# One drive of every second chunk goes from GpSimd to VectorE in a Mamba state-space loop

## The reference

```
xz = seq @ W_in.T ;  u, z = split(xz)
u = silu(causal_conv4(u) + conv_b)
dt = softplus(...) ;  Bmat, Cmat = rows of u @ W_x.T
h = exp(dt_t * A) * h + (dt_t * u_t) * B_t      # per channel and state
y = sum over states of h * C_t
out = (y + u * Dp) * silu(z) @ W_out.T
```

## Time and profile before

| | |
|---|---|
| median of 3 runs | 6102.17 us (6101.44 to 6105.2) |
| the profiled execution | 6112.24 us, span 6110.4 us |
| mean granted TensorE clock | 0.939 |
| state-space loop in the span | from about 75 to about 3714 us |
| busy over the span | PE 83%, DVE 80%, POOL 78%, ACT 55% |

### The profile page before, as it was taken

One profiled execution on the slowest core, in us unless ns is written; L12 is line 12 of the kernel. 1 busy time (PEld: TensorE's weight loads), 2 busy tenths in 40 slices (PEclk: granted clock), 3 DMA queues, 4 the chain that ended last, 5 costly groups with the idle time before them and its releaser, 6 DMA issues. The chain is left out here.

```text
span 6110.4 us, 72884 instructions
## 1 busy us (share of the span) xinstructions
PE 5081.1 (83%) x22486; PEld 2628.5 (43%) x22486; DVE 4908.9 (80%) x6708; ACT 3384.9 (55%) x4253; POOL 4779.0 (78%) x2219
## 2 busy tenths in 40 slices
PE   6888888888888888888888887972549989889897
PEld 2333333333433433433333334420326656566565
DVE  7999999999999999999999996006467677776665
ACT  4555565566566566555555552000437767667776
POOL 5999999999999999999999994000337767667676
PEclk8999999999999999999999998885879999999999
DMA  4555556555555555555555552681449999999999
GB/s 178 203 201 207 195 201 207 198 196 208 195 200 204 203 197 205 198 200 204 203 198 202 203 195 71 286 322 19 92 105 177 188 169 188 182 170 189 187 189 209
DMA packets 1424095, 1152.36 MB, mean 189 GB/s; under 512 B 1216728, under 2 KB 1226096, under 8 KB 1415792
## 3 DMA queue, kind: packets, MB, share of 16 engines
q1 hardware_dynamic: 1421330, 1149.30, 65.9%
q10 hardware_dynamic: 2528, 0.26, 0.0%
HBM read 814.23 MB, written 21.09 MB: 137 GB/s over the span
## 5 line engine op out<-in xcount | busy, mean ns | idle before, releaser
L871 POOL TENSOR_TENSOR mamba_state<-mamba_state,mamba_c_row 128x1024 f32<-128x1024 f32 x1024 | 2410.7, 2371 | 70.6 <-DVE mamba_state L831 62.5
L1750 POOL TENSOR_TENSOR l3s_el<-l3s_s_sb,l3s_eh 128x1024 f16<-128x1024 f32 (+2 forms) x584 | 1169.8, 2014 | 1121.0 <-ACT l3s_s_sb L1735 1113.5
L705 PE MATMUL mamba_y_ps<-mamba_state,ident 128*128 128x512 f32 x4096 | 1993.8, 613 | 40.6 <-POOL mamba_state L871 39.2
L831 DVE TENSOR_TENSOR_SCAN mamba_state<-mamba_decay,mamba_b_ps 128x1024 f32<-128x1024 f32 x704 | 1609.1, 2286 | 78.8 <-ACT mamba_b_ps L787 1.5
L705 PEld LDWEIGHTS mamba_y_ps<-mamba_state,ident 128*128 128x128 f32 x4096 | 780.4, 195 | 867.2 <-issue 681.1
L1758 DVE TENSOR_SCALAR_CACHE_REDUCE l3s_s_sb<-l3s_s_ps 128x512 f32<-128x512 f32 (+1 forms) x1096 | 753.5, 689 | 484.5 <-PE l3s_s_ps L1694 461.4
L1707 PE MATMUL l3s_o_ps<-l3s_vt,l3s_et 128*128 128x257 f16 x4368 | 878.3, 278 | 194.6 <-DMA l3s_et<-l3s_el 130.0
L1734 ACT ACTIVATE l3s_eh<-l3s_s_sb,l3s_shift 128x1024 f16<-128x1024 f32 (+2 forms) x584 | 634.5, 1087 | 541.8 <-DMA l3s_et<-l3s_el 441.3
L787 ACT ACTIVATE mamba_decay<-mamba_dt,mamba_A 128x1016 f32<-128x1016 f32 x704 | 791.7, 1133 | 235.5 <-POOL mamba_dt L852 167.0
L817 DVE TENSOR_TENSOR mamba_b_ps<-mamba_dtu,mamba_b_ps 128x1024 f32<-128x1024 f32 x704 | 850.8, 1209 | 30.8 <-PE mamba_b_ps L693 30.7
L693 PE MATMUL mamba_b_ps<-mamba_bc,mamba_pick 128*128 128x512 f32 x1408 | 571.9, 488 | 288.9 <-DVE mamba_state L831 282.2
(11 more groups left out here) (301 smaller groups left out, 5216.0 us busy)
## 6 DMA issues: line engine op xcount, KB each, us to landing
mamba_c_row<-mamba_c_rows SPq DMA_DIRECT2D x1024, 512.0 KB, 3.7
mamba_b_row<-mamba_c_rows SPq DMA_DIRECT2D x320, 512.0 KB, 4.8
l_ring_a<-in_L_conv_W SPq DMA_DIRECT2D x28, 1024.0 KB, 11.0
l2b_ring_b<-in_L_conv_W SPq DMA_DIRECT2D x26, 1024.0 KB, 11.1
mamba_xs<-X SPq DMA_DIRECT2D x64, 256.0 KB, 5.5
l_ring_a<-in_L_conv_W SPq DMA_DIRECT2D x14, 704.0 KB, 12.7
l2b_ring_b<-in_L_conv_W SPq DMA_DIRECT2D x13, 704.0 KB, 12.7
l_ring_a<-in_L_conv_W SPq DMA_DIRECT2D x14, 640.0 KB, 12.1
```

The costliest lines, as they stand in the source:

```text
L705: last = nc.tensor.matmul(y_ps[:, half(h)], C["ident"][:, :], state[:, s % STATES, half(h)], start=False, stop=(s == S - 1))
L831: nc.vector.tensor_tensor_scan(state[:, s % STATES, :], by, add, 0.0, ALU.mult, ALU.add).then_inc(s_scan, 1)
L871: nc.gpsimd.tensor_tensor(state[:, s % STATES, :], state[:, s % STATES, :], c_row[:, s % C_ROWS, :], ALU.mult).then_inc(s_hc, 1)
L1750: nc.gpsimd.tensor_tensor(el[:, part, off:off + EXPW], s_sb[:, par, j * EXPW:(j + 1) * EXPW], eh[:, part, off:off + EXPW], ALU.subtract).t ...
```

## The change

In odd chunks GpSimd's units are (2, 4, 6, 8) and no longer (2, 4, 6, 8, 10). Unit 10 of these 32 chunks is then made like any other of VectorE's: one-hot product on TensorE, drive on VectorE, decay into a `decay` tile. The one-hot blocks become twelve (`SPREAD`, the states that are VectorE's in some chunk). The counts that engines wait for go by a function `drives`, since the chunks no longer have equal numbers, and the row loads of slot 4 are counted per two chunks. To make room, `ImageNorm` keeps three slots in `norm_mine` and `norm_m2` instead of four, and `norm_var` shares the tile of `norm_minus`. The same instructions as before work on these.

```diff
-        self.mine = mem.sb("norm_mine", [P, B * G])
-        self.m2 = mem.sb("norm_m2", [P, B * G])
+        self.mine = mem.sb("norm_mine", [P, KEPT * G])
+        self.m2 = mem.sb("norm_m2", [P, KEPT * G])
...
-        self.var = mem.sb("norm_var", [P, G])
+        self.var = self.minus
...
+    def own(self, j):
+        return slice(j % KEPT * G, (j % KEPT + 1) * G)
...
-                for i, unit in enumerate(DVE_UNITS):
+                for i, unit in enumerate(SPREAD):
...
-POOL_UNITS = (2, 4, 6, 8, 10)
-DVE_UNITS = tuple(s for s in range(S) if s not in POOL_UNITS)
+POOL_UNITS = ((2, 4, 6, 8, 10), (2, 4, 6, 8))
+DVE_UNITS = tuple(tuple(s for s in range(S) if s not in units) for units in POOL_UNITS)
+SPREAD = tuple(s for s in range(S) if any(s in units for units in DVE_UNITS))
+
+
+def drives(units, c):
+
+    return (c + 1) // 2 * len(units[0]) + c // 2 * len(units[1])
...
-            return c * len(DVE_UNITS) + sum(1 for k in DVE_UNITS if k <= s)
+            return drives(DVE_UNITS, c) + sum(1 for k in DVE_UNITS[c % 2] if k <= s)
...
+        def b_loads(c, s):
+
+            return c + 1 if s in POOL_UNITS[1] else c // 2 + 1
...
-            if s in POOL_UNITS:
+            if s in POOL_UNITS[c % 2]:
                 return
             wait(pe, s_scan, unit + 1 - PAIRS)
...
-            if s in POOL_UNITS:
+            if s in POOL_UNITS[c % 2]:
                 wait(act, s_scan, unit + 1 - PAIRS)
...
         def dve_drive(dve, c, par, s):
-            if s in POOL_UNITS:
+            if s in POOL_UNITS[c % 2]:
                 return
...
-            wait(pool, s_brow[b_slot(s)], 16 * (c + 1))
+            wait(pool, s_brow[b_slot(s)], 16 * b_loads(c, s))
...
-            if s + B_LOAD_AHEAD in POOL_UNITS:
+            if s + B_LOAD_AHEAD in POOL_UNITS[c % 2]:
                 load_b(sp, c, par, s + B_LOAD_AHEAD)
...
-            if s + DRIVE_AHEAD in POOL_UNITS:
+            if s + DRIVE_AHEAD in POOL_UNITS[c % 2]:
                 pool_drive(pool, c, par, s + DRIVE_AHEAD)
```

More of the change, by code:

```diff
@@ L215, in vector_stats @@
     def vector_stats(self, dve, j):
-        nc, mine, m2 = self.nc, self.mine[:, self.groups(j)], self.m2[:, self.groups(j)]
+        nc, mine, m2 = self.nc, self.mine[:, self.own(j)], self.m2[:, self.own(j)]
         for g in range(G):
@@ L246, in scalar_stats @@
             act.wait_ge(self.s_first, G * (later + 1))
-            nc.scalar.activation(self.mine[:, self.groups(j)], self.sums[:, :], ACT.Identity,
+            nc.scalar.activation(self.mine[:, self.own(j)], self.sums[:, :], ACT.Identity,
                                  scale=0.5 / N).then_inc(self.s_centre, 1)
@@ L251, in scalar_stats @@
         wait(act, self.s_second, G * later + g)
-        at = j % B * G + g
+        at = j % KEPT * G + g
         nc.scalar.activation(over, group(g), ACT.Square, bias=self.minus[:, g:g + 1],
@@ L265, in sum @@
             src = (self.mine, self.m2)[k]
-            last = nc.tensor.matmul(ps[:, 0:G], self.C["one"][:, :], src[:, self.groups(j)], start=True, stop=True)
+            last = nc.tensor.matmul(ps[:, 0:G], self.C["one"][:, :], src[:, self.own(j)], start=True, stop=True)
         if k == 2:
@@ L310, in gpsimd @@
         nc, act_done, pool_done = self.nc, ACT_STEPS * j, POOL_STEPS * j
-        square, root, m2 = self.square[:, :], self.root[:, :], self.m2[:, self.groups(j)]
+        square, root, m2 = self.square[:, :], self.root[:, :], self.m2[:, self.own(j)]
         scale, bias = self.scale_g[:, self.groups(j)], self.bias_g[:, self.groups(j)]
@@ L314, in gpsimd @@
             pool.wait_ge(self.s_act, act_done + 1)
-            op = nc.gpsimd.tensor_tensor(self.dev[:, :], self.mine[:, self.groups(j)], self.mean[:, :], ALU.subtract)
+            op = nc.gpsimd.tensor_tensor(self.dev[:, :], self.mine[:, self.own(j)], self.mean[:, :], ALU.subtract)
         if i == 1:
@@ L333, in gpsimd @@
         op.then_inc(self.s_pool, 1)
-ACT_STEPS, POOL_STEPS = 10, 6
+ACT_STEPS, POOL_STEPS, KEPT = 10, 6, 3
 WEIGHTS = ("W_in", "conv_w", "conv_b", "W_x", "W_dt", "b_dt", "A_log", "Dp", "W_out")
@@ L608, in by_dve @@
         def by_dve(c, s):
-            return c * len(DVE_UNITS) + sum(1 for k in DVE_UNITS if k <= s)
+            return drives(DVE_UNITS, c) + sum(1 for k in DVE_UNITS[c % 2] if k <= s)
         def by_pool(c, s):
-            return c * len(POOL_UNITS) + sum(1 for k in POOL_UNITS if k <= s)
+            return drives(POOL_UNITS, c) + sum(1 for k in POOL_UNITS[c % 2] if k <= s)
         def b_slot(s):
-            return POOL_UNITS.index(s)
+            return POOL_UNITS[0].index(s)
+        def b_loads(c, s):
+            return c + 1 if s in POOL_UNITS[1] else c // 2 + 1
         def rows(h):
@@ L692, in pe_rows @@
             for h in range(2):
-                last = nc.tensor.matmul(b_ps[s % PAIRS][:, half(h)], C["pick"][:, DVE_UNITS.index(s) * P:(DVE_UNITS.index(s) + 1) * P],
+                last = nc.tensor.matmul(b_ps[s % PAIRS][:, half(h)], C["pick"][:, SPREAD.index(s) * P:(SPREAD.index(s) + 1) * P],
                                         bc[:, par, half(h)], start=True, stop=True)
@@ L741, in act_prep @@
                 wait(act, s_pbc, n + 1)
-                wait(act, s_b, len(DVE_UNITS) * (n - 1))
+                wait(act, s_b, drives(DVE_UNITS, n - 1))
                 nc.scalar.activation(bc[:, par, :], prep_ps[:, :], ACT.Copy).then_inc(s_hi, 1)
@@ L855, in pool_prep @@
                 wait(pool, s_u, n + 1)
-                wait(pool, s_drive, len(DVE_UNITS) * (n - 1))
-                wait(pool, s_bdrive, len(POOL_UNITS) * (n - 1))
+                wait(pool, s_drive, drives(DVE_UNITS, n - 1))
+                wait(pool, s_bdrive, drives(POOL_UNITS, n - 1))
                 nc.gpsimd.tensor_tensor(dtu[:, par, :], dt[:, par, :], u[:, :], ALU.mult).then_inc(s_dtu, 1)
         def pool_drive(pool, c, par, s):
-            if s == POOL_UNITS[0]:
+            if s == POOL_UNITS[0][0]:
                 wait(pool, s_dtu, c + 1)
-            wait(pool, s_brow[b_slot(s)], 16 * (c + 1))
+            wait(pool, s_brow[b_slot(s)], 16 * b_loads(c, s))
             row = b_row[:, b_slot(s), :]
@@ L970, in _ @@
                 for i in range(B_ROWS):
-                    sp.wait_ge(s_brow[i], 16 * TOTAL)
+                    sp.wait_ge(s_brow[i], 16 * b_loads(LAST, POOL_UNITS[0][i]))
             @block.tensor
@@ L2013, in program @@
         with Memory(nc, "mamba") as m:
-            C["pick"] = m.sb("pick", [P, len(DVE_UNITS) * P], fp32r)
+            C["pick"] = m.sb("pick", [P, len(SPREAD) * P], fp32r)
             Ms = [{"w_u": m.sb(f"w_u{i}", [P, TAPS * D]), "w_z": m.sb(f"w_z{i}", [P, D]), "w_dt": m.sb(f"w_dt{i}", [P, D]),
```

## The result

The changed kernel has a median of 6152.06 us (4 runs, 6146.53 to 6156.88) against 6101.81 for the kernel before (6100.37 to 6105.2): a ratio of 1.0084, 95% interval 1.0072 to 1.0095. It is slower by 50 us. The forecast was 6137 us, +35. The profiled execution took 6156.88 us, its span is 6155.1: 44.7 us more than the span before. (The profiled execution before lay 10 us above its median, that of after 5 us; hence 44.7 here and 50 there.)

What follows compares the result with a forecast made beforehand. VectorE's queue was taken to pace the state-space loop: added drives +35 us, its waits unchanged, everything else nothing, so 6137 us on the median of 6102.17. The range was 6110 to 6170 us.

Steps and rivals of the forecast that it cites:

- term for the drives: VectorE's added drive 10 in odd chunks: 31 x 1.12 us plus 0.3 in chunk 63, sum +35 us.
- VectorE's queue paces: State-space loop: VectorE's own queue sets the pace; GpSimd follows with no slack to spare but does not hold it.
- (A): Rival: GpSimd paces the loop and VectorE's waits are its lateness handed on; 6102 + 35 - 50 = 6087 us, chance 0.07.
- GpSimd's idling: GpSimd's idle before its products at L871 was to be about 180 us, against 70.6 before.
- Counts and norm tiles: Norm tiles kept for three images with one shared add no instruction or wait, and no cost: zero.
- ScalarE's earlier exponential: Unit 10's exponential goes into a decay slot, waiting for scan 6 instead of 8; nobody waits longer.
- the lighter DMA: SP's queue loses 32 row loads of 512 KB and their long-met wait: worth nothing.
- the twelfth one-hot copy: One more one-hot copy ahead of the loop, 0.2 us, counted as zero.
- I take them as unchanged: VectorE's 50 us of waits at drives, gate and scans stay as they are; bounds were -15 and +74 us.
- rival (C): Longer gap before z leaves TensorE at 1.2 GHz nearly every chunk: up to +74, 6176 us; half that excess 6156; chance 0.15.
- the gap before z: TensorE's idle before the z product at step 10 grows from 2.40 to about 2.95 us in odd chunks.
- The reason given for unchanged waits: Round trip from L805 to drive 11 against scan 10 is exactly the same; no row shows GpSimd's relief reaching the gate.

Runs made afterwards that it cites:

- e9: Kernel before, with one extra VectorE instruction ahead of u at step 4 of odd chunks, result to a free tile; 6148.57 us, ratio 1.0078.
- e4: Kernel before, with GpSimd's drive of unit 10 in odd chunks done on one column only, nothing added on VectorE; 6097.31 us, ratio 0.9992.
- e8: Change made twice: GpSimd has units (2, 4, 6, 8) in every chunk, against the kernel before; 6183.09 us, ratio 1.0129.
- e6: Changed kernel with two repeats of unit 11's one-hot product ahead of the z product at step 10; 6108.59 us, ratio 1.0007 to the kernel before.
- e10: Changed kernel with five GpSimd units in all chunks: all of the diff but the moved drive; 6104.21 us, ratio 1.0003 to the kernel before.
- e2: Changed kernel with the z product moved to step 11, behind unit 11's one-hot product; 6107.37 us, ratio 1.001 to the kernel before.
- e3: Changed kernel with a full-size GpSimd multiply on a free row replacing the lost drive in odd chunks; 6150.72 us, ratio 1.0083 to the kernel before.
- e5: Changed kernel, but VectorE takes over unit 8 instead of 10 in odd chunks; 6172.27 us, ratio 1.0114 to the kernel before.
- e11: Kernel before, with two repeats of unit 11's one-hot product ahead of the z product at step 10; 6076.38 us, ratio 0.9958.
- e1: Kernel before, with the z product moved from step 10 to step 11, behind unit 11's one-hot product; 6080.66 us, ratio 0.9966.

## Why the prediction was right, and where it fell short

The direction, its mechanism and the range held: +50 us against +35, within 6110 to 6170. The term for the drives was right to about 1 us; the term for VectorE's waits was not.

- VectorE's queue paces: shown. e9 adds 37 us of another instruction to it and costs 45; e4 takes 71 us from GpSimd and brings 4. With (A), GpSimd as the pace, e4 would have been at 6052.
- A drive ahead of L805 costs 1.12 us: 57.09 for an undisturbed chunk in e8 against 55.97, and in e6 even and odd chunks differ by 1.13. In the changed kernel itself only three odd chunks have no wait; they take 57.21 to 57.27.
- GpSimd's idling, forecast at about 180 us, is 184.8.
- Counts and norm tiles: zero, by e10. ScalarE's earlier exponential, the lighter DMA and the twelfth one-hot copy were not tried by themselves. The profile after shows no wait of VectorE for DMA in the loop's chunks, and for ScalarE 0.5 us, against 2.5 before.
- **The step that failed is "I take them as unchanged"**, of VectorE's 50 us of waits. In the profiled executions the waits at drive 11 grew from 30 to 51 us and those at the gate fell by 13; with those before scans the sum rose by 6. The first is rival (C), of which I had taken the upper end as 39 us more and gave 0.15. It came true by half. The second I had put at nothing. That +35 came as near as it did is in part luck: two errors of opposite sign. Filled (e6) or reordered (e2), the changed kernel loses 43 to 45 us of its time.
- The profile before understates the rise, since it was a long execution. e10 runs the same schedule as the kernel before, and its profile (6099.61 us) has 46.1 us of waits from first scan to last, where the change has 59.1: +13. With the 36 of the drives this makes 49, and the two loops differ by 51.1 (3624.9 and 3676.0). So of the measured 50 some 36 are the drives and some 13 the waits.
- Within that step a working was wrong: the gap before z was to be 2.95 us and is 3.33. I had sum 7 move by the length of the one-hot pair. But in the kernel before, sum 7 had itself waited for GpSimd's product 7 inside the record of eight (the product ends at 1410.74, the sum's first matmul starts at 1410.79), and the pair now fills that wait: TensorE is done 4.63 us after its one-hot product 9 (1425.81 to 1430.44), 4.43 before (1408.34 to 1412.77), and VectorE comes 1.12 later: 2.41 + 1.12 - 0.20 = 3.33.
- The reason given for unchanged waits, that the round trip is the same, holds only at a given clock. It was the clock, and what the engine did before it, that changed.
- The 6 us between +44.7 in the profiles and +50 in the medians are this same long execution: it took 6112.24 us, and 52 later ones of the same kernel, on three chips, lie between 6089.6 and 6111.8.

Open: why the gate's waits fell. They are small in the change (2.7), in e3 with GpSimd nearly full (3.3), in e5 (2.7) and in e4 with only the relief (5.9), but 11.0 in e8 and 14.3 in e9, so neither GpSimd's load nor longer chunks alone does it.

Open too is how the fall of the clock spreads over chunks. Without the long pause before z hardly any z product is slow (none of 63 in e6 and e11, 3 in e1); that a longer pause makes more of them slow is not shown. e8 has the long gap everywhere and fewer slow z products (34) than the change made once (41). In the change the slow ones went from 10 to 18 in even chunks, whose gap did not change, and from 9 to 23 in odd ones. And with one gap of 2.4 us throughout, the kernel before shows a pattern of its own: from chunk 20 to chunk 34 the z product takes about 2.1, then 1.4, then 1.1 us, over and over. Chunks 24 and 26, between and behind the two of the earlier trace rows:

```profile
1472.39 1.43 PE L682 MATMUL mamba_prep_ps<-mamba_xt,mamba_w_z 64*128 64x512 f32 x4 [2.40 <-DVE mamba_gu L805]
...
1585.82 2.08 PE L682 MATMUL mamba_prep_ps<-mamba_xt,mamba_w_z 64*128 64x512 f32 x4 [2.40 <-DVE mamba_gu L805]
```

So the length of the gap alone does not decide which z product is slow; when it falls in time matters too, and no run here separates the two.

## What to carry to other kernels

When two engines look equally full, look at who waits for whom, and price a moved instruction by its distance start to start on the engine that never waits for the other; here some 70 us off the one were worth nothing and 36 on the other were paid in full. Then look at the queue of the third engine for short products that stand behind long waits: here the clock was found halved just behind the pause, where VectorE waited for the next product. Moving the short product ahead of the wait, or filling the pause with repeats of a product that is due anyway, gave 21 to 27 us on a kernel whose two main engines were busy 96 and 98% of the loop. And profile the kernel before more than once before counting on its waits: two profiles of one schedule had 53 and 46 us of them.

## What the hardware showed beyond what I expected

After pauses of TensorE of 2.4 us between stretches of matmuls the next product took over 1.9 us in 19 of 63 chunks, with a granted clock of 0.50 to 0.55 over it; with 3.3 us in odd chunks it was 41, with 3.3 in all of them 34, with 3.8 in odd ones 53, and with repeats in the pause, which left some 1.3 us ahead of them, none. One and the same kernel varied by 22 us between 52 executions. The quickest had a mean granted clock of 0.941 to 0.943 and the longest one of 0.938 to 0.941, a tendency; that the clock makes the difference is not shown.
